# DLRM tower on one core: 11 table lookups instead of 12, halved subtractions, and the layer work in two sets of PSUM banks

## The reference

```python
e = jnp.stack([tbl_f[ids[:, f]] for f in range(27)], axis=1)      # (512, 27, 128)
z = jnp.einsum('bnd,bmd->bnm', e, e)[:, i, j]                      # i, j = triu_indices(27, k=1): 351 pairs
h = jnp.concatenate([z, dense_ctx], axis=1)                        # (512, 367)
h = jnp.maximum(h @ W_top1 + b_top1, 0.0)                          # 367 -> 512
h = jnp.maximum(h @ W_top2 + b_top2, 0.0)                          # 512 -> 256
y = h @ W_top3                                                     # 256 -> 1
```

## Time and profile before

| | us |
|---|---|
| median of 3 runs | 138.52 (138.08 to 139.58) |
| the profiled execution | 138.44 |
| its span, first to last instruction | 136.5 |
| busy in the span: PE / PEld / DVE / ACT / POOL | 116.4 / 93.8 / 77.6 / 65.2 / 76.3 |
| mean granted TensorE clock, share of full | 0.912 |

### The profile page before, as it was taken

The page is one execution under the profiler, slowest core; times in us unless marked ns, Lnnn a source line. Parts: engine busy times, 40 slices in busy tenths (PEclk is TensorE's granted clock), DMA queues, the critical chain, the costliest instruction groups (busy, mean ns, idle before and its releaser), DMA issues.

```text
span 136.5 us, 2480 instructions
## 1 busy us (share of the span) xinstructions
PE 116.4 (85%) x1016; PEld 93.8 (69%) x1016; DVE 77.6 (57%) x67; ACT 65.2 (48%) x106; POOL 76.3 (56%) x92
## 2 busy tenths in 40 slices
PE   5679989999698987989895697757899989999894
PEld 5546767777486775867674465535699969899791
DVE  2499999999999999999602020200435011531221
ACT  4099998999949696596030203002422111151021
POOL 2187888788788787888889989987000000001300
PEclk9999999999999999999999755555579999999999
DMA  3987787888675869941121112551144410003300
GB/s 58 325 340 175 245 255 243 275 199 264 225 237 168 243 143 362 352 94 38 38 56 44 38 38 58 179 102 53 45 126 111 106 27 0 0 5 130 74 0 1
DMA packets 15103, 18.67 MB, mean 137 GB/s; under 512 B 8767, under 2 KB 10905, under 8 KB 14964
## 3 DMA queue, kind: packets, MB, share of 16 engines
q1 hardware_dynamic: 12932, 14.20, 34.5%
q0 software_dynamic: 2016, 4.06, 10.6%
q10 hardware_dynamic: 144, 0.26, 1.1%
HBM read 16.74 MB, written 1.77 MB: 136 GB/s over the span
## 4 chain that ended last, share of the span: by engine, by line
PE 39%; DVE 36%; issue 16%; DMA 6%; ACT 1%; SPq 0%; ACTq 0%; DVEq 0%
DVE hot L432 24%; PE psG L332 18%; DVE parts L437 11%; PE psH L347 5%; PE psH L377 4%; DMA pick_ids<-in_picked_ids 3%; PE psT L295 3%; PE psG L315 3%; PE psG L359 3%; DMA pair_blocks<-gram 2%; PE psH L390 2%; DMA zT<-pair_blocks 1%; ACT gram L526 1%; DVE ET L422 1%; SPq L162 0%
## 5 line engine op out<-in xcount | busy, mean ns | idle before, releaser
L273 POOL DMA_INDIRECT rows<-in_tbl,ids_sb x60 | 65.4, 1090 | 19.7 <-issue 15.1
L315 PE MATMUL psG<-hot,parts 128*128 128x512 f32 x216 | 55.4, 403 | 7.4 <-DVE hot L432 2.9
L315 PEld LDWEIGHTS psG<-hot,parts 128*128 128x128 f32 x216 | 38.6, 188 | 20.8 <-DVE hot L432 6.5
L432 DVE TENSOR_TENSOR hot<-pick_ids,psH 128x1536 fp32r<-128x1536 int32 (+1 forms) x24 | 47.4, 2014 | 3.3 <-DMA pick_ids<-in_picked_ids 3.3
L332 PE MATMUL psG<-ET 128*52 128x54 f32 x512 | 25.1, 248 | 8.1 <-issue 7.0
L332 PEld LDWEIGHTS psG<-ET 128*52 128x52 f32 x512 | 20.6, 154 | 13.2 <-issue 11.8
L445 DVE COPY gram<-psG 128x432 f32<-128x432 f32 x8 | 7.2, 903 | 30.4 <-remote 19.8
L526 ACT COPY gram<-psG 128x432 f32<-128x432 f32 x8 | 7.2, 898 | 28.4 <-remote 19.8
L170 POOL DMA_DIRECT2D zT<-pair_blocks x2 | 1.7, 869 | 30.5 <-DMA pair_blocks<-gram 30.5
L437 DVE TENSOR_TENSOR parts<-table,parts 128x1024 fp32r<-128x1024 f32 (+1 forms) x12 | 16.2, 1352 | 0.0
L514 ACT ACTIVATE hot<-pick_ids,row_no 128x512 fp32r<-128x512 int32 x24 | 16.2, 727 | 0.0
(11 more groups left out here) (27 smaller groups left out, 40.5 us busy)
## 6 DMA issues: line engine op xcount, KB each, us to landing
table<-in_tbl SPq DMA_DIRECT2D x6, 640.0 KB
table<-in_tbl SPq DMA_DIRECT2D x6, 512.0 KB, 6.5
pick_ids<-in_picked_ids SPq DMA_DIRECT2D x11, 256.0 KB, 3.9
pair_blocks<-gram SPq DMA_DIRECT2D x8, 216.0 KB, 2.4
w_sb<-in_w SPq DMA_DIRECT2D x1, 1024.0 KB
rows<-in_tbl,ids_sb POOLq DMA_INDIRECT x60
w_sb<-in_w SPq DMA_DIRECT2D x1, 512.0 KB
zT<-pair_blocks SPq DMA_DIRECT2D x7, 63.0 KB
```

The costliest lines, as they stand in the source:

```text
L273: pool.indirect_dma_start(out=rows[:, n % RING, x, :], out_offset=None, in_=gathered_tables[f], in_offset=bass.IndirectOffsetOnAxis(ap=ids ...
L315: last = pe.matmul(psP[:, k % 2, :], parts[:, k % 2, x, c, :], hot[:, k % 2, c, :], start=x == 0 and c == 0, stop=x == 1 and c == CH[k] - 1)
L432: dve.tensor_tensor(hot[:, k % 2, first:end, :], pick_ids[:, k % TABLES, :].unsqueeze(1).to_broadcast(shape), numbers.unsqueeze(2).to_broa ...
```

## The change

It does several things:

- `PICKED` is 11: one table of 1,250 rows is gathered instead of looked up. There are 64 gathers in 16 quads of 4.
- `BY_ACT` is 3 for the tables of 10 chunks. ACT's Relu is one instruction over all its chunks.
- The subtraction is made in two halves, each behind one of the two comparisons (`hot_and_low`); PE takes high and low part of a group of chunks together (first 3 chunks, the rest of DVE's, then ACT's).
- Behind every gather POOL fills 4 columns (`PAUSE = 4`), from the first gather on.
- ACT writes half of each tile to scratch (`write_half`), and reads two chunks of tile 0 and one of tile 3 (`read_half`).
- Layer 1 of tile 0 goes chunk by chunk in `psG`, as do its layers 2 and 3; the list `steps` is rearranged around it.

The diff, cut to its core:

```diff
-    BY_ACT = [2] * FP
+    BY_ACT = [2 if chunks == min(CH) else 3 for chunks in CH]
-    PAUSE = 320
-    FIRST_PAUSED = 10
+    PAUSE = 4
-    DUE = [2, 3, 4, 5, 6, 7, 9, 10, 11]
+    DUE = [2, 3, 4, 5, 6, 7, 8, 9, 10]
+    BY_CHUNK = (0, T - 1)
+    SP_READS = [(0, 1), (0, 1, 2, 3), (0, 1, 2, 3), (0, 2)]
+    ACT_READS = [(2, 3), (), (), (1,)]
...
-        steps = units(0) + quads(9, 10) + units(1) + quads(10, 12) + units(2) + quads(12, 13)
-        steps += mlp(0) + quads(13, 14) + [("layer3", 0)] + mlp(1) + quads(14, 16) + [("layer3", 1)] + units(3)
-        steps += mlp(2) + [("chunk", 0), ("layer3", T - 2), ("chunk", 1), ("chunk", 2),
+        steps = units(0) + [("write", 0)] + quads(9, 10) + units(1) + [("write", 1)] + quads(10, 11) + [("read", 0)]
+        steps += quads(11, 12) + units(2) + [("write", 2)] + mlp(0) + quads(12, 14)
+        steps += [("layer1", 1), ("layer3", 0), ("layer2", 1), ("layer2_end", 1)] + quads(14, 16) + [("layer3", 1)]
+        steps += units(3) + [("write", 3)]
+        steps += mlp(2) + [("read", T - 1), ("chunk", 0), ("layer3", T - 2), ("chunk", 1), ("chunk", 2),
...
-                for x in range(S):
-                    write_blocks(sp, t, x)
+                write_blocks(sp, t, 0)
...
-                    if n >= FIRST_PAUSED:
-                        if pauses:
-                            pool.wait_ge(paused, pauses)
-                        pool.memset(pause[:, :], 0.0).then_inc(paused, 1)
-                        pauses += 1
+                    if pauses:
+                        pool.wait_ge(paused, pauses)
+                    pool.memset(pause[:, :], 0.0).then_inc(paused, 1)
+                    pauses += 1
 
             pool.wait_ge(blocks_out[T - 1], 16 * S)
             read_pairs(pool, T - 1, 3)
-            read_pairs(pool, T - 1, 1)
...
+                own = CH[k] - BY_ACT[k]
+                groups = (range(HOT_SPLIT), range(HOT_SPLIT, own), range(own, CH[k]))
+                for g, pieces in enumerate(groups):
...
+                    for x in range(2):
+                        for c in pieces:
+                            if x == 0 and c == 0 and k == 0:
+                                pe.wait_ge(first_half_ready, 1)
+                            elif x == 0 and c == (CH[k] // 2 if k == 0 else 0):
+                                pe.wait_ge(high_ready, k + 1)
+                            elif x == 1 and c in (0, CH[k] // 2):
+                                pe.wait_ge(low_ready, 2 * k + (1 if c == 0 else 2))
...
+            def layer1_chunk(t, c):
 
                 if c == 0:
-                    pe.wait_ge(gram_dve, U * T)
-                    pe.wait_ge(gram_act, U * T)
+                    products = U * (T if t == T - 1 else T - 1)
+                    pe.wait_ge(gram_dve, products)
+                    pe.wait_ge(gram_act, products)
...
+            def hot_and_low(k):
...
+                for x, (first, end) in enumerate(((0, HOT_SPLIT), (HOT_SPLIT, own))):
...
+                    a, b = (half, CH[k]) if x else (0, half)
+                    if k == 0 and x == 0:
+                        dve.wait_ge(first_half_ready, 1)
+                    else:
+                        dve.wait_ge(high_ready, k + 1)
+                    dve.tensor_tensor(parts[:, k % 2, 1, a:b, :], table[:, k % TABLES, a:b, :],
+                                      parts[:, k % 2, 0, a:b, :], ALU.subtract).then_inc(low_ready, 1)
...
-                for x, c in enumerate(chunks):
-                    act.wait_ge(distance_ready, sum(BY_ACT[:k]) + x + 1)
-                    act.activation(hot[:, k % 2, c, :], hot[:, k % 2, c, :], ACT.Relu, bias=1.0, scale=-1.0
-                                   ).then_inc(last_hot_ready, 1)
+                act.wait_ge(distance_ready, sum(BY_ACT[:k + 1]))
+                last = hot[:, k % 2, chunks[0]:CH[k], :]
+                act.activation(last, last, ACT.Relu, bias=1.0, scale=-1.0).then_inc(last_hot_ready, 1)
...
+            def write_half(t):
+                act.wait_ge(gram_dve, U * (t + 1))
+                act.wait_ge(gram_act, U * (t + 1))
+                write_blocks(act, t, 1)
+
+            def read_half(t):
+                act.wait_ge(blocks_out[t], 16 * S)
+                for c in ACT_READS[t]:
+                    read_pairs(act, t, c)
...
-PICKED = 12
+PICKED = 11
```

More of the change, by code:

```diff
@@ L225, in _ @@
                     sp.wait_ge(hot_ready, 2 * (k - TABLES + 1))
-                    sp.wait_ge(last_hot_ready, sum(BY_ACT[:k - TABLES + 1]))
+                    sp.wait_ge(last_hot_ready, k - TABLES + 1)
                 if k >= 1:
@@ L245, in _ @@
                 sp.wait_ge(gram_act, U * (t + 1))
-                for x in range(S):
-                    write_blocks(sp, t, x)
+                write_blocks(sp, t, 0)
                 sp.wait_ge(blocks_out[t], 16 * S)
-                for c in range(NC) if t < T - 1 else (0, 2):
+                for c in SP_READS[t]:
                     read_pairs(sp, t, c)
@@ L300, in pick @@
                     pe.wait_ge(picked_out, k - 1)
-                for x, ready in enumerate((high_ready, low_ready)):
-                    if k == 0 and x == 0:
-                        pe.wait_ge(first_half_ready, 1)
-                    else:
[L305 to L316, removed]
+                own = CH[k] - BY_ACT[k]
+                groups = (range(HOT_SPLIT), range(HOT_SPLIT, own), range(own, CH[k]))
+                for g, pieces in enumerate(groups):
+                    if g < 2:
+                        pe.wait_ge(hot_ready, 2 * k + g + 1)
+                    else:
+                        pe.wait_ge(last_hot_ready, k + 1)
+                    for x in range(2):
[6 more added lines that the diff above has]
+                                pe.wait_ge(low_ready, 2 * k + (1 if c == 0 else 2))
+                            last = pe.matmul(psP[:, k % 2, :], parts[:, k % 2, x, c, :], hot[:, k % 2, c, :],
+                                             start=x == 0 and c == 0, stop=x == 1 and c == CH[k] - 1)
                 last.then_inc(picked, 1)
@@ L350, in layer1 @@
                         last.then_inc(l1_done, 1)
[L352 removed]
+            def layer1_chunk(t, c):
                 if c == 0:
[L355 to L357 removed]
+                    products = U * (T if t == T - 1 else T - 1)
+                    pe.wait_ge(gram_dve, products)
+                    pe.wait_ge(gram_act, products)
+                if c == 0 and t == 0:
+                    pe.wait_ge(w1_in, 16)
+                    pe.wait_ge(dense_in, 16)
+                pe.wait_ge(chunk_in[t][c], 16 * len(CHUNKS[c]))
                 for n in ORDER:
[L359 to L360 removed]
+                    last = pe.matmul(h1_psum(t, n), w1_sb[0:ROWS[c], c, P * n:P * (n + 1)],
+                                     zT[0:ROWS[c], t, c, :], start=c == 0, stop=c == NC - 1)
                     if c == NC - 1:
@@ L384, in layer3 @@
                     pe.wait_ge(small_in, 48)
+                elif t < T - 1:
+                    pe.wait_ge(y_ready, t)
                 for k in range(N2):
@@ L405, in _ @@
                     transposes(x)
+                elif step == "layer1" and x in BY_CHUNK:
+                    for c in range(NC):
+                        layer1_chunk(x, c)
                 elif step == "layer1":
@@ L427, in make_hot @@
                     dve.wait_ge(picked, k - 1)
+                half = CH[k] // 2
                 own = CH[k] - BY_ACT[k]
-                for first, end in ((0, HOT_SPLIT), (HOT_SPLIT, own)):
+                for x, (first, end) in enumerate(((0, HOT_SPLIT), (HOT_SPLIT, own))):
                     shape = [V, end - first, B]
@@ L557, in _ @@
                     quad_copy(x)
+                elif step == "write":
+                    write_half(x)
+                elif step == "read":
+                    read_half(x)
                 elif step in ("layer1", "relu1"):
```

33 lines of the change are left out of this document (14 added, 19 removed).

## The result

The changed kernel takes **158.31 us** (157.46 to 158.92, 4 runs), the kernel before 138.30 (137.89 to 139.58, 4 runs, same measurement): ratio **1.145 [1.140, 1.150]**. The forecast was 128.0 us; the change costs 20.0 us.

A forecast was written before the change was run, and what follows sets the result against it. DVE was taken to bound until about 67 us, PE from 70.51, not by its arithmetic. Tile 2's products ending at 91.6, plus 34.44 for the rest, gave 126.1; plus 1.94, 128.0 us; range 125.0 to 134.5.

The forecast's parts named there:

- Lookups: Table lookups: one 10-chunk table less, five with 512 columns less on DVE; first unit at 62.75 us, 7.76 us earlier.
- Units 0 to 3: Products beside gathers: PE takes 13 records per gather, 10.7 a us, and ends these units at 83.6 us.
- DVE's pace: DVE in the lookups: 1.042 ns a column plus 0.065 us an instruction; 10-chunk tables 5.33 us, last subtraction at 59.3.
- no cost for ACT: Lookups: ACT makes the high part some 2 us ahead, so costed at nothing; up to 1.4 us otherwise.
- Gathers: POOL's 64 gathers: 1.22 us apart, halved subtractions catching fewer (some 8); last ends at 88.0 us, within 86 to 90.
- PE's pace is its own: Rival on products beside gathers: PE's pace stays 8.75 records a us; 131.7 us in all; chance 0.20.
- The long fill was PE's air: Rival on products beside gathers, lower bound: without the long fill 5.4 records a us; 133.7 us; chance 0.12.
- PE is freed: Rival on products beside gathers, upper bound: about 20 records a us; 121.6 us; chance 0.08.
- ACT's issues: Before tile 2's products: ACT issues one write and three reads ahead of quad 11's copy; 1.6 us added.
- The copy before layer 1: Layer 1 of tile 0 waits for the last copy of the products; 1.1 us added.
- The rest: From the end of tile 2's products to the span's end: 34.44 us, against 33.84 before.
- Slower: Rival: "The long fill was PE's air" plus half clock in the layers; 140.4 us, or 147; chance 0.07.

The follow-up runs named there:

- whole form: Changed kernel with one subtraction a table, behind both comparisons, instead of halves: 116.85, 116.56 and 116.61 us free; 159.49 us held up without fills.
- second and third experiment: Kernel before without its 320-column fills: 141.06 us, 1.017; kernel before with fills of 4 columns instead of 320: 142.35 us, 1.026.

## Why the prediction was wrong

**The step that failed is "Lookups"**, and in it what it left out. It was worked out from DVE's columns, with PE ("20 x 0.23 + 0.45 = 5.1 us of work a table: hidden") and PE's signals taken as prompt. The hold-up of PE beside gathers was in the trace, and the prediction priced it, but for "Units 0 to 3" alone, since only there did the rows of before show it. It did not ask why the same gathers did PE no harm in the lookups. The next step had one possible answer, booked as a gain: "Halved subtractions catch fewer gathers". If catching them was what spaced POOL out, as B has it, the change took it away; that part is not shown. What the runs show is that PE's signals, priced at nothing, came 5.5 and 31.8 us late. The forecast had the last subtraction at 59.3 and the first product at 62.75; held up they came at 101.7 and 105.24, **42.5 us later**.

The loss may feed itself: once a signal of PE is late DVE stops, no subtraction then makes a gather longer, and POOL goes on at one gather in 1.26 us, until about 43 us.

That the change is faster when free, as forecast, is in part luck: the forecast was worked out for a PE that is held up beside the units, and free it is not.

The other terms:

- **DVE's pace** was right wherever PE isn't held up: free, the last subtraction ends at 59.46 and the first product starts at 62.99, against 59.3 and 62.75. So "no cost for ACT" was right too. (The 5.6 us of ACT a table should read 5.5 by the prediction's own terms.)
- **Gathers**: the fill of 4 columns takes 0.12 to 0.13 us, the gap behind it 0.19; a period of 1.26 for a forecast 1.22. Free, the last gather ends at 89.1, inside 86 to 90.
- **Units 0 to 3** were not put to the test held up, as the gathers were over by then (128 records in 3.32 us at 105.24). Free, there is no hold-up to price. "PE's pace is its own" falls all the same: held up, PE's pace followed the fill (second and third experiment), 13 records a gather with the long one and 1 to 5 with none. The Trainium skill's rule (SBUF — State Buffer, "Who interferes with whom") that PE never waits on another engine does not describe these held-up traces. "The long fill was PE's air" was the right idea, seen in the kernel before alone. The sum of "PE is freed" is 0.4 us short, since 128 records at 20 a us take 6.4.
- **ACT's issues**: PE waits 2.98 us before tile 2's products, where it was 0.62: 2.4 more for a forecast 1.6. **The copy before layer 1**: 1.10 us, as forecast. **The rest**, from the end of tile 2's products (120.53): 35.1 us for a forecast 34.4. Both rows:

```profile
116.40 4.89 PE L339 MATMUL psG<-ET 128*52 128x54 f32 x128 [2.98 <-issue]
...
122.39 2.80 PE L367 MATMUL psG<-zT,w_sb 126*128 126x128 f32 x23 [1.10 <-DVE gram L459]
```

- **Slower** had 0.07, by a clock that stays low in the layers. It was slower by something else, so that chance was no foresight, and the range rested on cases that all took the lookups for settled.
- Free, the change gave 5.6% for a forecast 7.6%. The first product moved by 7.64 us (forecast 7.76), but from there on the changed kernel took 52.3 us of its span of 115.3, the one before 48.7 of 119.3: the wait for gathers and the low clock at tile 2.

**What stays open**: what makes one measurement held up and another free, by what path gathers reach PE and the signals, if it is the gathers at all, and what besides the halves brings the stand into the changed kernel. One rival no run tests: that the recording of the trace does it. Every execution on record has its span and granted clock, so no time is known to have been taken without recording. The held-up traces lack a third to a half of their semaphore records, PE's last records before it stands (29.74 to 34.65 us) start 0.70 us apart whether they are weight loads or matmuls, and POOL's signals are late too. No version beat the kernel before in a held-up measurement; in free ones the changed kernel as it is had the lowest time, within the noise of its whole form.

## What to carry to other kernels

Where a wait ends long after the instruction that it is for, follow it back to the late signal before calling any engine slow. When a trace shows one engine held up beside another's work, ask of every stage in which both run why it is or is not held up there, before taking away anything that slows the second engine. A stall on an engine that isn't the bound (here POOL's 0.8 us behind DVE's subtraction) may be what keeps the bound moving; here that was neither shown nor refuted. And run the kernel before beside every variant: the sign of this change turned with the measurement.

## What the runs showed of the hardware

- The same program took 138 to 139 us or 121 to 123 us, and what differs is PE beside gathers: 8.75 records a us against 39. The held-up traces lack many of their semaphore records: the kernel before has 1,586, the changed one 1,251, where the free traces of both have 2,416 and 2,458, for some 2,480 instructions. They are fewest where the lookups stand (1,223 to 1,530 in six traces) against 1,586 to 1,631 in the three where only the units are held up.
- Held up, a matmul's signal reached its waiter up to 41.6 us after the matmul's recorded end (the changed kernel with long fills), while a gather of POOL's still took its usual 0.95 us. Signals stayed out even for 5.6 us in which no gather was being issued and the DMA engines were 5% busy.
- A fill of 320 columns (0.38 us) behind each gather of quads 10 to 15 is worth 2.4 us to the kernel before when held up (138.62 with it, 141.06 without), and costs 3.0 in the whole form of the changed kernel when free (119.84 against 116.85 with 4 columns behind each gather).
